# Two banks in turn for the dense product of a graph layer, and the compare tables moved from PSUM to SBUF

## The chip, the cores and the metric

The kernel runs on one core of a Trainium2 chip, as one program. The metric is the time of one execution on the device, in microseconds (us). The engines of the core are TensorE (PE in the rows, and PEld for its weight loads), VectorE (DVE), ScalarE (ACT), GpSimd (POOL) and SyncE (SP). SBUF is the working memory; PSUM has eight banks of 2 KB in each partition, which TensorE writes and which VectorE and ScalarE read.

## The reference

One layer of a graph network with two kinds of edges, then a residual and a layer norm. There are 12,500 nodes of 128 features and 400,000 edges, sorted by their target node.

```
Xs  = X[src]                                   # (400000, 128)
msg = where(edge_types == 0, Xs @ W_data.T + b_data, Xs @ W_control.T + b_control)
agg = segment_sum(msg, dst, num_segments=12500)
h   = relu(agg + (X @ W_self.T + b_self))
out = layernorm(X + h, axis=-1, eps=1e-05)     # no scale, no shift
```

The kernel uses that the sum over edges can come before the products with the weights: for each node and edge kind it sums the source rows, and then multiplies the sums.

## The kernel before

**Three parts of x.** TensorE multiplies two-byte numbers, so x is split in three bf16 parts (high, middle, low). `x3` keeps them side by side in SBUF, 98 blocks of 128 rows by 385 columns (3 x 128 and a column of ones, which counts edges). A copy of them, `x3_dram`, serves the gathers. The split is made in the load phase, up to about 73 us, on ScalarE (L813, L823) and VectorE (L1147, L1163).

**The dense part** covers the first 5632 nodes, in 88 blocks of 64 nodes (x 2 kinds = 128 columns). For a block a matrix of counts is made: how often each of the 12,500 source nodes occurs among the edges of each target and kind. It is made in eight batches. `make_onehots(n)` (VectorE, L1136) compares the keys of edges with tables of running numbers and writes one-hots: `hot_p` (512 two-byte elements in a partition) and `hot_q` (784). `build(n)` (TensorE, L648) multiplies the one-hots into the banks of `build_ps`, in two halves; `evacuate(n)` (ScalarE, L860) copies the counts to `cnt` in two activations. `cnt` holds two blocks in turn. `apply(k, c)` (TensorE, L664) multiplies an eighth of block k's counts with `x3` and adds up all 98 products in one bank, `apply_ps`. Then `post(k)` (VectorE, L1210 and L1211) reads the bank into `zd` and `sd` and raises `posted`. `turn_block(k)` turns the sum two steps later, and `take_block` (ScalarE) stores it.

**The sparse part** covers the other nodes, in 173 rounds of ten tiles of 128 edges. GpSimd gathers the source rows by index (L560), ten gathers a round, into 20 slots, two rounds ahead; within a round it waits at four places for later batches of `build`, so that the gathers are spread out. `make_hot(ps)` (VectorE, L1041) makes a one-hot of the targets inside windows of 32 nodes, by comparing keys with the table `HOT`; in the first 12 rounds it and the gathered rows are float. `gather_sums` (TensorE, L630, in the first 12 rounds L627) sums the rows; `add_parts` (L1191, L1193) and `add_sums` (L1181, L1183) on VectorE bring them to the accumulators.

**Order.** All engines run the same list of 700-odd steps, written out ahead. In a step TensorE does at most one `gather_sums`, one `build`, one small turn or output in the bank `misc`, and one eighth of an `apply`. The x products of block k start at step 8 + 8k. VectorE does the `post` of the block before at the start of the same step, then the sums, then `make_onehots` for three steps later.

**PSUM before.** `const_ps` holds constants (the table `HOT` as floats, and the tables for `hot_p` and `hot_q` as bf16 numbers, each stored twice in a row), `build_ps` takes four banks, `apply_ps`, `sum_ps` and `misc` one each. All eight are in use. The x products of a block wait for the read of the block before:

```
                if c == 0:
                    pe.wait_ge(evacuated, 16 * (k + 1))
                    if k:
                        pe.wait_ge(posted, k)
```

Of the kernel before, what the change touches and what calls it, by code (L numbers as in the profile page):

```python
# [12 lines left out]
ALU = mybir.AluOpType  # L13
# [36 lines left out]
def gnn_resnorm(nc, x, src, dst, etype, w_data, b_data, w_ctrl, b_ctrl, w_self, b_self, out):  # L50
# [116 lines left out]
    with ctx:  # L167
# [20 lines left out]
        hot_p = sb("hot_p", [P, 8, P, 2], BF16)  # L188
        hot_q = sb("hot_q", [P, 8, 2 * XBLOCKS, 2], BF16)
        src_t = sb("src_t", [P, GROUPS * GT], I32)  # L190
        key_t = sb("key_t", [P, GROUPS * GT])
# [64 lines left out]
        def region(b0, nb, dt):  # L256
# [31 lines left out]

        const_ps = psum("const_ps")
        build_ps = [psum(f"build{i}", 2 * WIDE) for i in range(2)]  # L290
        apply_ps = psum("apply_ps")
        sum_ps = psum("sum_ps")
        misc = psum("misc")
        end_ps = [build_ps[1][:, 0:D], build_ps[1][:, WIDE:WIDE + D], build_ps[0][:, WIDE:WIDE + D],
                  apply_ps[:, 0:D]]
        HOT = slice(0, 2 * WIN)
        TABLES = slice(2 * WIN, 2 * WIN + P + 2 * XBLOCKS)
        tables = const_ps[:, TABLES].bitcast(BF16).rearrange("p (w r) -> p w r", r=2)
        table_p, table_q = tables[:, 0:P, :], tables[:, P:P + 2 * XBLOCKS, :]
        twice = start_hot[:, :, :].rearrange("p k n -> p (k n)").bitcast(BF16)[:, 0:2 * (P + 2 * XBLOCKS)].rearrange(  # L300
            "p (w r) -> p w r", r=2)

# [281 lines left out]
        def _(pe):  # L584
# [24 lines left out]
            for k in range(3):  # L609
                last = pe.transpose(apply_ps[:, k * D:(k + 1) * D], w_nat[:, k, :], ident[:, :])  # L610
            last.then_inc(weights_turned, 1)
# [40 lines left out]
            def apply(k, c):  # L652

                if c == 0:
                    pe.wait_ge(evacuated, 16 * (k + 1))
                    if k:
                        pe.wait_ge(posted, k)
                    if k == 0:
                        pe.wait_ge(wt_ready, 1)
                b0, b1 = XBLOCKS * c // 8, XBLOCKS * (c + 1) // 8  # L660
                if k == 0:
                    pe.wait_ge(x3_ready, -(-b1 // XB))
                for b in range(b0, b1):
                    last = pe.matmul(apply_ps[:, 0:385], cnt[:, k % 2, b, :], x3[:, b, 0:385],  # L664
                                     start=(b == 0), stop=(b == XBLOCKS - 1))
                if c == 7:
                    last.then_inc(applied, 1)
# [100 lines left out]
            with pe.If(general > 0):  # L768
                with pe.Fori(0, TILES) as t:
                    pe.wait_ge(late_gathered, (t + 1) * 16)  # L770
                    pe.transpose(misc[:, 0:P], late_x, ident[:, :]).then_inc(late_turned, 1)
                    pe.wait_ge(late_xt_ready, t + 1)
                    pe.matmul(apply_ps[:, 0:2 * D], late_xt, w_t[:, 1:3, :].rearrange("p k d -> p (k d)"),
                              start=True, stop=True).then_inc(late_both_ready, 1)
                    with pe.Fori(0, WINDOWS) as w:
                        pe.wait_ge(late_hot_ready, t * WINDOWS + w + 1)
                        pe.matmul(sum_ps[:, 0:LW], late_msg, late_hot, start=True, stop=True
                                  ).then_inc(late_summed, 1)
                pe.wait_ge(late_added, TILES * WINDOWS)
                for u in range(LATE_UNITS):  # L780
                    i = UNITS + u
                    r = late_rows(u)
                    pe.wait_ge(y_ready, i)
                    pe.wait_ge(late_bias_loaded, 32 + 16 * (u + 1))
                    pe.transpose(misc[:, 0:r], x_u[0:r, 1, :], ident[0:r, 0:r]).then_inc(late_turned, 1)
                    pe.wait_ge(late_xt_ready, TILES + u + 1)
                    pe.matmul(apply_ps[0:r, 0:D], x_t[:, 1, 0:r], w_t[:, 0, :], start=True, stop=False)
                    pe.matmul(apply_ps[0:r, 0:D], acc_all[:, u * P:u * P + r], ident[:, :],
                              start=False, stop=False)
                    pe.matmul(apply_ps[0:r, 0:D], fin_deg[:, 0, 0:r], bias3[:, :], start=False, stop=True  # L790
                              ).then_inc(late_both_ready, 1)
# [3 lines left out]
        def _(act):  # L795
# [102 lines left out]
            for c in range(FIRST_X):  # L898
                split_hi(c)
                if c:  # L900
                    split_mid(c - 1)
                if c == 1:
                    act.wait_ge(weights_turned, 1)
                    act.activation(w_t[:, :, :].rearrange("p k d -> p (k d)"), apply_ps[:, 0:3 * D],
                                   ACT.Copy).then_inc(wt_ready, 1)
                if c == 2 or c == 3:
                    store_lists(c - 1)
# [59 lines left out]
        def _(dve):  # L967
# [53 lines left out]
            dve.wait_ge(iota_done, 5)  # L1021
            dve.tensor_copy(const_ps[:, HOT], hot_i[:, :])
            twice_p, twice_q = twice[:, 0:P, :], twice[:, P:P + 2 * XBLOCKS, :]
            for r in range(2):
                dve.tensor_copy(twice_p[:, :, r], iota_q[:, 0:P])
                last = dve.tensor_single_scalar(twice_q[:, :, r], iota_q[:, :], 1.0, ALU.add)
            step(last)
            dve.tensor_copy(const_ps[:, TABLES], twice.rearrange("p w r -> p (w r)").bitcast(F32))
            step(dve.tensor_copy(iota_n[:, :], iota_i[:, :]))

            def make_hot(ps):
# [5 lines left out]
                elif 2 * ps % P == 0:  # L1037
# [3 lines left out]
                dve.tensor_tensor(to[:, ps % 3, :, :],  # L1041
                                  const_ps[:, HOT].unsqueeze(1).to_broadcast([P, 2 * GT, 2 * WIN]),
                                  keys.unsqueeze(2).to_broadcast([P, 2 * GT, 2 * WIN]),
# [161 lines left out]
            def post(k):  # L1205

                dve.wait_ge(applied, k + 1)
                if k:
                    dve.wait_ge(misc_full, job[block_step[k - 1]] + 1)
                dve.tensor_tensor(zd[:, :], t_mask[:, 1, :], apply_ps[:, 384:385].to_broadcast([P, 2]), ALU.mult)  # L1210
                dve.tensor_reduce(sd[:, :], apply_ps[:, 0:384].rearrange("p (k d) -> p d k", k=3), AX.X, ALU.add  # L1211
                                  ).then_inc(posted, 1)
# [114 lines left out]
            with dve.If(general > 0):  # L1327
# [7 lines left out]
                with dve.Fori(0, TILES) as t:  # L1335
# [6 lines left out]
                    dve.wait_ge(late_both_ready, t + 1)  # L1342
                    dve.tensor_tensor(late_both[:, 0:D], apply_ps[:, 0:D], sd[:, :], ALU.add)
                    dve.tensor_tensor(late_both[:, D:2 * D], apply_ps[:, D:2 * D], late_bias, ALU.add
                                      ).then_inc(late_step, 1)
# [20 lines left out]
                for u in range(LATE_UNITS):  # L1366
                    i = UNITS + u
                    dve.wait_ge(late_both_ready, TILES + u + 1)
                    dve.wait_ge(out_ready, i - 1)
                    residual(i, late_rows(u), apply_ps, 1)  # L1370
                    moments(i, late_rows(u))
# [21 lines left out]
```

## Time and profile before

| | |
|---|---|
| time, median of 3 runs | 2782.12 us (2778.26 to 2785.72) |
| time of the profiled execution | 2784.88 us |
| its span, first to last instruction | 2783.0 us |
| TensorE, matmuls | 2364.6 us busy (85%) |
| GpSimd | 1691.7 us (61%) |
| VectorE | 1266.1 us (45%) |
| ScalarE | 1224.5 us (44%) |
| mean granted clock of TensorE | 0.96 of full speed |

The span is the time in which instructions run; the profiled execution takes 1.9 us more. An engine's busy time is a sum over its instructions. Matmuls are pipelined and their ends are modelled, so the busy time of TensorE is no measure of how near it is to its peak. Idle time of an engine is listed with what ended it; "issue" means that the profile shows nothing that it waited for, "remote" a release that the profile can't place.

### The profile page before, as it was taken

What the parts mean: (1) busy time and instruction counts of PE and PEld (TensorE: products, weight loads), DVE (VectorE), ACT (ScalarE), POOL (GpSimd) and SP (SyncE); (2) the same over time, 40 slices, a digit from 0 to 9 for tenths busy, and PEclk for the clock granted to TensorE, in tenths of its full rate; (3) what the DMA queues carried; (4) which work ended last, traced back from release to release, by engine and by line L of the source; (5) the groups of instructions that cost most, each with busy time, mean ns of one, the idle gap of its engine ahead of it and who ended that gap; (6) DMA issues with size and microseconds to landing.
All of it is one profiled execution on the core that took longest, in us unless ns stands there. A gap on an engine that the chain in (4) does not pass through costs nothing.

```text
span 2783.0 us, 47819 instructions
## 1 busy us (share of the span) xinstructions
PE 2364.6 (85%) x17776; PEld 1301.3 (47%) x17776; DVE 1266.1 (45%) x4037; ACT 1224.5 (44%) x1997; POOL 1691.7 (61%) x1785
## 2 busy tenths in 40 slices
PE   3688888888888888888889888988888888888988
PEld 2344444544444444444445454444444444444444
DVE  8444444445444444444444454444444444444443
ACT  6344444444444444444444444444444444444443
POOL 6466665666666665666666666566666666656662
PEclk9899999999999999999999999999999999999999
DMA  7712222222222222222222222222222222222221
GB/s 191 223 47 67 71 72 59 73 68 74 72 73 71 73 72 62 74 69 75 71 72 73 69 75 71 63 69 73 74 69 73 71 73 72 69 61 72 71 75 34
DMA packets 150380, 211.42 MB, mean 76 GB/s; under 512 B 35298, under 2 KB 120725, under 8 KB 150147
## 3 DMA queue, kind: packets, MB, share of 16 engines
q0 software_dynamic: 83232, 170.57, 22.0%
q1 hardware_dynamic: 54177, 28.15, 3.7%
q10 hardware_dynamic: 12738, 9.60, 1.1%
q8 instruction: 145, 2.38, 0.3%
q14 instruction: 88, 0.72, 0.1%
HBM read 189.78 MB, written 18.41 MB: 75 GB/s over the span
## 4 chain that ended last, share of the span: by engine, by line
PE 44%; another core or an unknown queue 23%; ACT 14%; DVE 9%; issue 7%; DVEq 2%; DMA 1%; SPq 0%; ACTq 0%
PE apply_ps L664 25%; ACT cnt L860 13%; PE build L648 8%; PE sum_ps L630 4%; DVEq L1177 2%; DVE hot_q L1136 2%; DVE hot_p L1136 1%; PE misc L673 1%; DVE acc L1183 1%; PE misc L714 1%; DVE sg L1193 1%; PE misc L717 1%; DMA key_dram<-fin 1%; PE misc L692 1%
## 5 line engine op out<-in xcount | busy, mean ns | idle before, releaser
L560 POOL DMA_INDIRECT rows<-x_dram,src_t x1610 | 1524.7, 947 | 947.5 <-issue 383.4
L860 ACT ACTIVATE cnt<-build 128x784 bf16<-128x784 f32 x1408 | 1087.5, 822 | 1457.1 <-remote 773.1
L664 PE MATMUL apply_ps<-x,cnt 128*128 128x385 bf16 x8624 | 1611.2, 337 | 31.0 <-issue 25.5
L664 PEld LDWEIGHTS apply_ps<-x,cnt 128*128 128x128 bf16 x8624 | 868.3, 103 | 604.7 <-issue 135.7
L648 PE MATMUL build<-hot_q,hot_p 64*128 64x196 bf16 x5632 | 425.1, 254 | 274.2 <-ACT cnt L860 205.6
L648 PEld LDWEIGHTS build<-hot_q,hot_p 64*128 64x128 bf16 x5632 | 197.6, 95 | 572.7 <-issue 372.7
L1136 DVE TENSOR_TENSOR hot_q<-const_ps,key_pq 128x784 bf16<-128x784 bf16 x704 | 390.3, 554 | 0.0
L1181 DVE TENSOR_TENSOR acc_deg<-misc,acc_deg 2x32 f32 x346 | 61.9, 179 | 671.2 <-remote 278.7
L1136 DVE TENSOR_TENSOR hot_p<-const_ps,key_pq 128x512 bf16<-128x512 bf16 x704 | 291.2, 414 | 43.1 <-DVE acc L1183 16.5
L560 POOL DMA_INDIRECT rows<-in_x,src_t x120 | 122.8, 1024 | 76.8 <-issue 30.5
L1191 DVE TENSOR_TENSOR zg<-t_mask,sum_ps 128x2 f16<-128x2 f32 x161 | 24.9, 154 | 307.5 <-PE sum_ps L630 158.3
L630 PE MATMUL sum_ps<-rows,hot 128*64 128x385 bf16 x1610 | 162.5, 331 | 0.0
L1216 DVE SCALAR_TENSOR_TENSOR y_sb<-misc,x_u 128x128 f32<-128x128 f32 (+3 forms) x105 | 30.4, 290 | 268.1 <-PE misc L717 163.9
L1041 DVE TENSOR_TENSOR hot<-const_ps,key_t 128x640 bf16<-128x640 f32 (+1 forms) x173 | 140.9, 814 | 0.0
L630 PEld LDWEIGHTS sum_ps<-rows,hot 128*64 128x64 bf16 x1610 | 77.1, 108 | 76.7 <-issue 52.1
L1193 DVE TENSOR_REDUCE sg<-sum_ps 128x128 f32<-128x384 f32 x161 | 88.7, 551 | 0.0
L1183 DVE TENSOR_TENSOR acc<-misc,acc 128x64 f32 x346 | 77.7, 225 | 2.1 <-issue 2.1
L1210 DVE TENSOR_TENSOR zd<-t_mask,apply_ps 128x2 f16<-128x2 f32 x88 | 13.6, 155 | 127.2 <-remote 45.6
L673 PE MATMUL misc<-ident,sg 128*128 128x128 f32 x173 | 58.8, 340 | 0.0
L692 PE MATMUL misc<-ident,x_u 128*128 128x128 f32 (+3 forms) x105 | 35.0, 333 | 27.1 <-DVEq L1186 14.3
L672 PE MATMUL misc<-picks,zg 128*2 128x64 f16 x173 | 33.2, 192 | 25.9 <-DVEq L1099 19.4
L537 POOL DMA_INDIRECT key_raw<-key_dram,key_at x44 | 41.8, 949 | 21.5 <-issue 13.1
(182 smaller groups left out, 1082.5 us busy)
## 6 DMA issues: line engine op xcount, KB each, us to landing
rows<-x_dram,src_t POOLq DMA_INDIRECT x1610
x_dram<-x ACTq DMA_DIRECT2D x13, 672.0 KB
cnt<-in_x SPq DMA_DIRECT2D x13, 448.0 KB
x_u<-in_x SPq DMA_DIRECT2D x43, 64.0 KB
out<-out_sb SPq DMA_DIRECT2D x43, 64.0 KB
key_dram<-fin SPq DMA_DIRECT2D x12, 196.5 KB
x_u<-in_x SPq DMA_DIRECT2D x40, 53.5 KB
out<-out_sb SPq DMA_DIRECT2D x40, 53.5 KB
```

Of the source, the lines that this page charges most:

```text
L560: pool.indirect_dma_start(out=rows_f[:, slot, 0:D] if early else rows[:, slot, 0:ROW], out_offset=None, in_=x if early else x3_dram, in_of ...
L630: last = pe.matmul(sum_ps[part, 0:ROW + 1], hot_b[:, ps % 3, st, :], rows[:, slot, 0:ROW + 1], start=(j == 0), stop=(j == GT - 1))
L648: last = pe.matmul(build_ps[z][:, o:o + 2 * XBLOCKS], hot_p[half, slot, :, i], hot_q[half, slot, :, i], start=True, stop=True)
L664: last = pe.matmul(apply_ps[:, 0:385], cnt[:, k % 2, b, :], x3[:, b, 0:385], start=(b == 0), stop=(b == XBLOCKS - 1))
L673: pe.transpose(misc[:, 0:P], sg[:, ps % 2, 0:D], ident[:, :]).then_inc(misc_full, 1)
L692: pe.transpose(misc[:, 0:v.r], x_u[0:v.r, i % 3, :], ident[0:v.r, 0:v.r]).then_inc(misc_full, 1)
L860: act.activation(o, i.rearrange("p h (m b) -> p b h m", b=XBLOCKS), ACT.Copy).then_inc(evacuated, 1)
L1041: dve.tensor_tensor(to[:, ps % 3, :, :], const_ps[:, HOT].unsqueeze(1).to_broadcast([P, 2 * GT, 2 * WIN]), keys.unsqueeze(2).to_broadcast( ...
L1136: last = dve.tensor_tensor(to[:, z:z + 2, :, :], table.unsqueeze(1).to_broadcast([P, 2, w, 2]), keys.unsqueeze(2).to_broadcast([P, 2, w, 2 ...
L1181: dve.tensor_tensor(dw, misc[0:2, P + 32 * g:P + 32 * g + 32], dw, ALU.add)
L1183: dve.tensor_tensor(aw, misc[:, 64 * g:64 * g + 64].rearrange("p (t w) -> p t w", t=2), aw, ALU.add).then_inc(acc_step, 1)
L1193: dve.tensor_reduce(sg[:, ps % 2, 0:D], sum_ps[:, 0:ROW].rearrange("p (k d) -> p d k", k=3), AX.X, ALU.add).then_inc(sg_ready, 1)
```

## The change

1. `apply_ps` becomes two banks. Block k uses bank k % 2, and its first product waits for the read of block k - 2. `post(k)` reads bank k % 2. All other users take bank 0.
2. `const_ps` goes, which frees the bank for this. The table `HOT` moves to the SBUF tile `hot_t`, the bf16 tables to the SBUF tile `tables`. Both compares, L1136 and L1041, then have two inputs in SBUF: a table and the keys.
3. In the set-up the bf16 tables are written straight into `tables`. Before, they were made in a spare part of `start_hot` and copied to the bank.

The gathers of three parts (rows of 384 two-byte numbers) stay as they are.

```diff
+        hot_t = sb("hot_t", [P, 2 * WIN])
+        tables = sb("tables", [P, P + 2 * XBLOCKS, 2], BF16)
...
-        const_ps = psum("const_ps")
         build_ps = [psum(f"build{i}", 2 * WIDE) for i in range(2)]
-        apply_ps = psum("apply_ps")
+        apply_ps = [psum(f"apply{i}") for i in range(2)]
...
-        tables = const_ps[:, TABLES].bitcast(BF16).rearrange("p (w r) -> p w r", r=2)
         table_p, table_q = tables[:, 0:P, :], tables[:, P:P + 2 * XBLOCKS, :]
...
-                    if k:
-                        pe.wait_ge(posted, k)
+                    if k >= 2:
+                        pe.wait_ge(posted, k - 1)
...
-                    last = pe.matmul(apply_ps[:, 0:385], cnt[:, k % 2, b, :], x3[:, b, 0:385],
+                    last = pe.matmul(apply_ps[k % 2][:, 0:385], cnt[:, k % 2, b, :], x3[:, b, 0:385],
...
-            dve.tensor_copy(const_ps[:, HOT], hot_i[:, :])
-            twice_p, twice_q = twice[:, 0:P, :], twice[:, P:P + 2 * XBLOCKS, :]
+            dve.tensor_copy(hot_t[:, :], hot_i[:, :])
             for r in range(2):
-                dve.tensor_copy(twice_p[:, :, r], iota_q[:, 0:P])
-                last = dve.tensor_single_scalar(twice_q[:, :, r], iota_q[:, :], 1.0, ALU.add)
-            step(last)
-            dve.tensor_copy(const_ps[:, TABLES], twice.rearrange("p w r -> p (w r)").bitcast(F32))
+                dve.tensor_copy(table_p[:, :, r], iota_q[:, 0:P])
+                dve.tensor_single_scalar(table_q[:, :, r], iota_q[:, :], 1.0, ALU.add)
             step(dve.tensor_copy(iota_n[:, :], iota_i[:, :]))
...
-                                  const_ps[:, HOT].unsqueeze(1).to_broadcast([P, 2 * GT, 2 * WIN]),
+                                  hot_t[:, :].unsqueeze(1).to_broadcast([P, 2 * GT, 2 * WIN]),
...
-                dve.tensor_tensor(zd[:, :], t_mask[:, 1, :], apply_ps[:, 384:385].to_broadcast([P, 2]), ALU.mult)
-                dve.tensor_reduce(sd[:, :], apply_ps[:, 0:384].rearrange("p (k d) -> p d k", k=3), AX.X, ALU.add
+                dve.tensor_tensor(zd[:, :], t_mask[:, 1, :], apply_ps[k % 2][:, 384:385].to_broadcast([P, 2]), ALU.mult)
+                dve.tensor_reduce(sd[:, :], apply_ps[k % 2][:, 0:384].rearrange("p (k d) -> p d k", k=3), AX.X, ALU.add
                                   ).then_inc(posted, 1)
```

## Rows read from the trace of the kernel before

**Rows 1.** The page, busy time of each engine over the span

```profile
PE 2364.6 (85%) x17776; PEld 1301.3 (47%) x17776; DVE 1266.1 (45%) x4037; ACT 1224.5 (44%) x1997; POOL 1691.7 (61%) x1785
```

**Rows 2.** The page, the chain that ended last, by engine and by line

```profile
PE 44%; another core or an unknown queue 23%; ACT 14%; DVE 9%; issue 7%; DVEq 2%; DMA 1%; SPq 0%; ACTq 0%
PE apply_ps L664 25%; ACT cnt L860 13%; PE build L648 8%; PE sum_ps L630 4%; DVEq L1177 2%; DVE hot_q L1136 2%; DVE hot_p L1136 1%; PE misc L673 1%; DVE acc L1183 1%; PE misc L714 1%; DVE sg L1193 1%; PE misc L717 1%; DMA key_dram<-fin 1%; PE misc L692 1%
```

**Rows 3.** Groups by line and form: count, busy us, mean ns, idle before

```profile
L664 PE MATMUL apply_ps<-x,cnt 128*128 128x385 bf16 x8624 | 1611.2, 337 | 31.0 <-issue 25.5 <-DVE sd L1211 4.0 <-ACT cnt L860 1.4
...
L1136 DVE TENSOR_TENSOR hot_q<-const_ps,key_pq 128x784 bf16<-128x784 bf16 x704 | 390.3, 554 | 0.0
L1136 DVE TENSOR_TENSOR hot_p<-const_ps,key_pq 128x512 bf16<-128x512 bf16 x704 | 291.2, 414 | 43.1 <-DVE acc L1183 16.5 <-remote 8.7 <-issue 7.7
L630 PE MATMUL sum_ps<-rows,hot 128*64 128x385 bf16 x1610 | 162.5, 331 | 0.0
L1041 DVE TENSOR_TENSOR hot<-const_ps,key_t 128x640 bf16<-128x640 f32 x161 | 131.1, 814 | 0.0
```

**Rows 4.** Timeline around 1530: start, duration, engine, operation, idle before

```profile
1528.36 2.31 PE L664 MATMUL apply_ps<-x,cnt 128*128 128x385 bf16 x13
...
1530.60 1.01 PE L630 MATMUL sum_ps<-rows,hot 128*64 128x385 bf16 x10
...
1532.91 0.16 DVE L1210 TENSOR_TENSOR zd<-t_mask,apply_ps 128x2 f16<-128x2 f32 x1 [1.70 <-remote]
1532.99 0.55 DVE L1211 TENSOR_REDUCE sd<-apply_ps 128x128 f32<-128x384 f32 x1
1533.14 1.54 ACT L860 ACTIVATE cnt<-build 128x784 bf16<-128x784 f32 x2 [3.92 <-PE build L648]
...
1533.69 2.14 PE L664 MATMUL apply_ps<-x,cnt 128*128 128x385 bf16 x12 [0.98 <-issue]
...
1535.76 0.53 PE L648 MATMUL build<-hot_q,hot_p 64*128 64x196 bf16 x8
```

**Rows 5.** Timeline around 1258, TensorE and then ScalarE

```profile
1258.54 2.14 PE L664 MATMUL apply_ps<-x,cnt 128*128 128x385 bf16 x12 [2.25 <-issue]
1260.61 0.53 PE L648 MATMUL build<-hot_q,hot_p 64*128 64x196 bf16 x8
...
1258.00 1.54 ACT L860 ACTIVATE cnt<-build 128x784 bf16<-128x784 f32 x2 [4.13 <-remote]
```

**Rows 6.** Waits of TensorE: total us, times, longest us

```profile
PE build L648 <- ACT cnt L860: 205.6, 296, 4.8
...
PE apply_ps L664 <- issue: 25.5, 24, 2.2
```

**Rows 7.** Timeline in the load phase, VectorE and then GpSimd

```profile
41.81 1.13 DVE L1147 TENSOR_TENSOR cnt<-cnt,x 128x896 f32<-128x896 f32 x1
42.89 1.07 DVE L1163 TENSOR_TENSOR x<-cnt,x 128x896 bf16<-128x896 f32 x1
...
41.82 0.95 POOL L560 DMA_INDIRECT rows<-in_x,src_t  x1 [0.30 <-issue]
43.07 1.70 POOL L560 DMA_INDIRECT rows<-in_x,src_t  x1 [0.30 <-issue]
```

**Rows 8.** Timeline around 1526, compares and one gather

```profile
1525.60 0.81 DVE L1041 TENSOR_TENSOR hot<-const_ps,key_t 128x640 bf16<-128x640 f32 x1
1525.78 0.95 POOL L560 DMA_INDIRECT rows<-x_dram,src_t  x1 [0.81 <-PE build L648]
...
1526.66 0.55 DVE L1136 TENSOR_TENSOR hot_q<-const_ps,key_pq 128x784 bf16<-128x784 bf16 x1
```

**Rows 9.** Timeline of GpSimd, one round of ten gathers

```profile
1502.85 0.95 POOL L560 DMA_INDIRECT rows<-x_dram,src_t  x1 [0.30 <-issue]
...
1516.44 0.94 POOL L560 DMA_INDIRECT rows<-x_dram,src_t  x1 [0.30 <-issue]
```

**Rows 10.** The gathers: duration ns min/median/max, first and last start

```profile
L560 POOL DMA_INDIRECT rows<-x_dram,src_t x1610: 941/947/1066, 216.7 to 2737.1; - x179
```

More of the change, by code:

```diff
@@ L294, in gnn_resnorm @@
         end_ps = [build_ps[1][:, 0:D], build_ps[1][:, WIDE:WIDE + D], build_ps[0][:, WIDE:WIDE + D],
-                  apply_ps[:, 0:D]]
-        HOT = slice(0, 2 * WIN)
-        TABLES = slice(2 * WIN, 2 * WIN + P + 2 * XBLOCKS)
-        tables = const_ps[:, TABLES].bitcast(BF16).rearrange("p (w r) -> p w r", r=2)
+                  apply_ps[0][:, 0:D]]
         table_p, table_q = tables[:, 0:P, :], tables[:, P:P + 2 * XBLOCKS, :]
-        twice = start_hot[:, :, :].rearrange("p k n -> p (k n)").bitcast(BF16)[:, 0:2 * (P + 2 * XBLOCKS)].rearrange(
-            "p (w r) -> p w r", r=2)
         lists_loaded = [sem(f"lists_loaded{i}") for i in range(len(LISTS))]
@@ L609, in _ @@
             for k in range(3):
-                last = pe.transpose(apply_ps[:, k * D:(k + 1) * D], w_nat[:, k, :], ident[:, :])
+                last = pe.transpose(apply_ps[0][:, k * D:(k + 1) * D], w_nat[:, k, :], ident[:, :])
             last.then_inc(weights_turned, 1)
@@ L772, in _ @@
                     pe.wait_ge(late_xt_ready, t + 1)
-                    pe.matmul(apply_ps[:, 0:2 * D], late_xt, w_t[:, 1:3, :].rearrange("p k d -> p (k d)"),
+                    pe.matmul(apply_ps[0][:, 0:2 * D], late_xt, w_t[:, 1:3, :].rearrange("p k d -> p (k d)"),
                               start=True, stop=True).then_inc(late_both_ready, 1)
@@ L786, in _ @@
                     pe.wait_ge(late_xt_ready, TILES + u + 1)
-                    pe.matmul(apply_ps[0:r, 0:D], x_t[:, 1, 0:r], w_t[:, 0, :], start=True, stop=False)
-                    pe.matmul(apply_ps[0:r, 0:D], acc_all[:, u * P:u * P + r], ident[:, :],
+                    pe.matmul(apply_ps[0][0:r, 0:D], x_t[:, 1, 0:r], w_t[:, 0, :], start=True, stop=False)
+                    pe.matmul(apply_ps[0][0:r, 0:D], acc_all[:, u * P:u * P + r], ident[:, :],
                               start=False, stop=False)
-                    pe.matmul(apply_ps[0:r, 0:D], fin_deg[:, 0, 0:r], bias3[:, :], start=False, stop=True
+                    pe.matmul(apply_ps[0][0:r, 0:D], fin_deg[:, 0, 0:r], bias3[:, :], start=False, stop=True
                               ).then_inc(late_both_ready, 1)
@@ L903, in _ @@
                     act.wait_ge(weights_turned, 1)
-                    act.activation(w_t[:, :, :].rearrange("p k d -> p (k d)"), apply_ps[:, 0:3 * D],
+                    act.activation(w_t[:, :, :].rearrange("p k d -> p (k d)"), apply_ps[0][:, 0:3 * D],
                                    ACT.Copy).then_inc(wt_ready, 1)
@@ L1342, in _ @@
                     dve.wait_ge(late_both_ready, t + 1)
-                    dve.tensor_tensor(late_both[:, 0:D], apply_ps[:, 0:D], sd[:, :], ALU.add)
-                    dve.tensor_tensor(late_both[:, D:2 * D], apply_ps[:, D:2 * D], late_bias, ALU.add
+                    dve.tensor_tensor(late_both[:, 0:D], apply_ps[0][:, 0:D], sd[:, :], ALU.add)
+                    dve.tensor_tensor(late_both[:, D:2 * D], apply_ps[0][:, D:2 * D], late_bias, ALU.add
                                       ).then_inc(late_step, 1)
@@ L1369, in _ @@
                     dve.wait_ge(out_ready, i - 1)
-                    residual(i, late_rows(u), apply_ps, 1)
+                    residual(i, late_rows(u), apply_ps[0], 1)
                     moments(i, late_rows(u))
```

## The prediction

> **What bounds the kernel now.** I read the page's busy line first, then the chain that ended last, then the groups by line and form, then single stretches of the timeline. TensorE is busy 2364.6 us of the 2783.0 us span, far above the 1266.1 us of VectorE, 1224.5 us of ScalarE and 1691.7 us of GpSimd [rows 1]. The chain agrees: 44% of it is TensorE, the product with x at L664 alone 25%, ScalarE's evacuation at L860 13%, VectorE 9% [rows 2]. So what TensorE waits for sets the time, and the other engines matter through the waits that they end.
>
> Two such waits touch this change. Before the first x product of a block, TensorE idles 31.0 us in all, of which only 1.4 us is put down to the evacuation [rows 3]. The stretches show what the part called "issue" is: at 1532.7 TensorE has finished its last turn, VectorE reads the products of the block before (zd at 1532.91, sd until 1533.54), and only at 1533.69 do the products of the new block start, 0.98 us idle [rows 4]. Near 1258 the same takes 2.25 us [rows 5]. The reason is the one bank: `apply(k, 0)` waits for `posted`. The read itself is late because its release arrives late: the old products end at 1530.67 (2.31 us from 1528.36), and zd starts at 1532.91, 2.2 us later.
>
> The second wait is the build waiting for the evacuation: 205.6 us in 296 waits [rows 6]. The change does not touch it, and it is where time freed before L664 can go.
>
> **Part 1: x products in two banks.** Nothing is added: same 8624 matmuls, same 88 pairs of zd and sd, other addresses. The wait of block k is now for the read of block k-2, which is some 30 us old at that point, so it should cost nothing. Ceiling: 31.0 - 1.4 = 29.6 us [rows 3]. What is late next? In the first stretch, the following build starts at 1535.76 and needs both evacuations, which ran 1533.14 to 1534.68. There is 1.08 us to spare, so the 0.98 us are kept whole. In the second, the build at 1260.61 needs the evacuations that end at 1259.54: 1.07 us of the 2.25 us are kept, or somewhat more where the second half is later [rows 4, 5]. Together they keep 2.05 of 3.23 us, or 63%. The first kind is the commoner one: 24 waits share 25.5 us and the longest is 2.2 us, a mean of 1.06 us [rows 3, 6]. Keeping 98% of a typical wait and half of a long one, I take 75% as the share: 29.6 x 0.75 = 22 us. The bounds of this term are 0 (every microsecond moves to the evacuation wait) and 30 us.
>
> VectorE gets no new wait. The read of block k stays where it was in its program, and `turn_block` still comes two steps later. TensorE may now run ahead of the read, but no further than the evacuations let it.
>
> **Part 2: tables to SBUF, VectorE's own time.** The instructions are hot_p (414 ns), hot_q (554 ns), 704 of each, and hot (814 ns), 161 plus 12 of the float form [rows 3]. Their second input, the keys, lies in SBUF already; now both inputs do. What does the place of an input cost? The float compare of 640 elements from the bank takes 814 ns; the float subtraction of 896 with both inputs in SBUF takes 1.07 to 1.13 us [rows 3, 7]. Taking elements off at the slope between the two, (1.07 - 0.814)/256 = 1.0 ns each, both leave a fixed 0.17 us. So I take no change, 0 us. The two-byte compares do 784 elements in 554 ns and 512 in 414 ns, which is 0.51 ns an element: two at a time, from a bank. Their form is kept, so I keep the rate. If it were lost, each step would pay (512 + 784) x 0.5 = 0.65 us, 704 x 0.65 = 457 us of VectorE time; bounds 0 to 457 us of engine time, of which little is on the path.
>
> The Trainium skill (VectorE: DVE Perf Modes, section "The perf-mode tier table") says that a tensor_tensor reads two-byte data two at a time from SBUF but one at a time when an operand is in PSUM. By that rule, as an estimate from its figures, hot_q should take over 0.9 us now and little more than half of it with this change. The trace has 554 ns already, so the measurement decides, and no gain is counted.
>
> **Part 3: tables to SBUF, GpSimd.** This is the cost to look for. In the load phase VectorE runs instructions with both inputs in SBUF, and there the gathers show what that does. The subtraction L1163 starts at 42.89 and ends at 43.96; the gather that starts under it, at 43.07, lasts 1.70 us in place of 0.95 and ends 0.81 us after the subtraction [rows 7]. In contrast, the compare L1041 from the bank starts at 1525.60 and the gather of 1525.78 keeps its 0.95 us [rows 8]. So a gather that begins under a VectorE instruction with two SBUF inputs waits for its end. After the change every compare is of that kind.
>
> The size: the compares are busy 291.2 + 390.3 + 131.1 = 813 us, 29% of the span [rows 3]. So some 29% of the 1610 gathers [rows 10], about 470, begin under one. The extension is what is left of the compare less 0.14 us (0.81 after its end against 0.95 in all); with half a compare left (0.2 to 0.4 us) that is 0.15 to 0.25 us, or 70 to 120 us of GpSimd over the kernel, 0.6 us in a round of ten gathers. If a waiting gather is passed over by compares that follow at once, it waits for the rest of a run. The run from the hot of 1525.60 to the end of the hot_q at 1527.21 lasts 1.6 us [rows 8], and a pair may stand before it; half of it is 0.8 us, and I take 0.9 us: 420 us in all, or 2.6 us a round.
>
> What hides it: the ten gathers of one round go out from 1502.85 to 1517.38, and TensorE adds them up at 1530.60 [rows 4, 9]. That is over 13 us to spare, and TensorE's sums L630 show no idle at all before them [rows 3]. A round lasts 15.7 us on average (from 216.7 to 2737.1 us, 1610 gathers, 161 rounds [rows 10]), and ten gathers 1.25 us apart (0.95 and 0.30) need 12.5 us [rows 9], so even 2.6 us more fit. I take 0 us on the path.
>
> The Trainium skill (SBUF — State Buffer, section "Who interferes with whom") gives the rule behind these rows: VectorE with two SBUF inputs holds a read port that GpSimd needs as well, and the second to come waits in full. The trace agrees (1.70 us for 0.95). Its list also supposes that a tensor_tensor doesn't stall descriptor making; here L1163 does.
>
> The other way round, L1147 starting 0.01 us before a gather takes 1.13 us, where L1163 with as many elements takes 1.07 [rows 7]. At 0.06 us for the few compares that begin in so narrow a window, 5% of 1581, this is 5 us of VectorE time, 0 on the path; if all paid it would be 95 us, of which the 9% share of VectorE on the chain [rows 2] makes 9 us. In the set-up one copy of 324 words goes (0.5 us at the rate above) with the wait in front of it: taken as 1 us.
>
> **Sum.** -22 (waits) - 1 (set-up) + 0 = -23 us. The profiled execution took 2784.9 us, 1.9 above its span: 2762. The median of runs is 2782.1, 2.8 less, which gives 2759; as the small charges on VectorE and GpSimd can only add, I say 2761.
>
> **Rivals.**
> *The wait only moves.* Releases from TensorE come late, as zd shows (2.2 us after the products' end [rows 4]); if the pause before L664 is what lets them catch up, ScalarE starts its evacuation just as much later and the build waits instead. For it: 205.6 us of build waits [rows 6], and the 4.13 us that ScalarE idles until 1258.00 while TensorE is idle too [rows 5]. Against it: the spare 1.08 us. Time: 0 to 8 us gained, 2778. Chance 0.24.
> *GpSimd becomes the bound (slower).* One mechanism: gathers starved by runs of compares. It decides once a round costs more than 15.7 us, that is 3.2 us more than 12.5. If half the gathers meet a run at 0.9 us, it is 4.5 us a round, 1.3 us too much, x 161 = 209 us slower; just past the point, 0.1 to 0.3 us a round is 16 to 48 us, around 2815. For it: the 1.70 us of [rows 7]. Against: 2.6 us is my upper estimate and 13 us of lead absorb short rounds. Chance 0.10.
> *VectorE slower.* The compares lose their two-at-a-time rate or wait for GpSimd more than thought. Their 3% of the chain (83 us) [rows 2] would grow by 0.65/0.97 = 67%, +56 us, less 23 gained: 2815. Chance 0.05.
> *The change does more than the sum.* TensorE never pauses, the long waits are kept whole too, and VectorE's chain moves up: 35 to 45 us, 2742. Chance 0.08.
> Forecast: 0.53.
>
> **Numbers.** A change of under 0.3%, 8 us, can't be told from none here. The forecast's own range is 2752 to 2772. To leave out no more than 2 in 10 the range must take in the moved wait (up to 2782 and a little of the slower side) and half of the larger gain: 2742 to 2788. Faster: 0.50 of the forecast, 0.08 of the larger gain, 0.05 of the moved wait: 0.63. Same: 0.19 of the moved wait, 0.03 of the forecast's slow edge, 0.02 where a small cost on GpSimd cancels the gain: 0.24. Slower: 0.08 + 0.05 = 0.13.
>
> **What would show it.** Right: idle before L664 falls from 31.0 us to under 4; zd still starts up to 2 us after its products, now without TensorE waiting; gathers in the steady part have a mean above 1.0 us and a maximum of 1.3 us or more, with none before the sums L630; hot_p and hot_q stay at 414 and 554 ns within 15. The wait of the build for L860 grows from 205.6 us by under 10. Wrong: that wait grows by 20 us or more (moved), idle appears before L630 (GpSimd), or the compares' means rise.

## The result: slower, and the profile after

The changed kernel takes 2802.8 us (median of 3, 2799.3 to 2806.2) against 2782.1 us before: a ratio of 1.0075, 95% interval 1.0045 to 1.0104. It is 20.7 us slower, where 21 us faster was forecast; the time lies outside the range.

Three more groups by line and form of the kernel before, to be read with [rows 3]:

```profile
L560 POOL DMA_INDIRECT rows<-x_dram,src_t x1610 | 1524.7, 947 | 947.5 <-issue 383.4 <-remote 270.3 <-PE build L648 159.6
L860 ACT ACTIVATE cnt<-build 128x784 bf16<-128x784 f32 x1408 | 1087.5, 822 | 1457.1 <-remote 773.1 <-PE build L648 643.6 <-issue 37.2
...
L648 PE MATMUL build<-hot_q,hot_p 64*128 64x196 bf16 x5632 | 425.1, 254 | 274.2 <-ACT cnt L860 205.6 <-issue 45.0 <-DVE hot_q L1136 17.2
```

The busy times of the engines and then the same groups of the kernel after. The lines have moved: L660 is L664 of before, L644 was L648, L1129 was L1136, L1034 was L1041, L626 was L630, L556 was L560, L856 was L860.

```profile
PE 2385.4 (85%) x17776; PEld 1307.5 (47%) x17776; DVE 1275.1 (45%) x4036; ACT 1222.2 (44%) x1997; POOL 1781.5 (64%) x1785
...
L660 PE MATMUL apply<-x,cnt 128*128 128x385 bf16 x8624 | 1633.3, 340 | 2.2 <-issue 2.2
L556 POOL DMA_INDIRECT rows<-x_dram,src_t x1610 | 1609.4, 1000 | 888.5 <-issue 402.4 <-remote 250.7 <-PE sum_ps L626 127.2
...
L644 PE MATMUL build<-hot_q,hot_p 64*128 64x196 bf16 x5632 | 426.9, 256 | 306.7 <-ACT cnt L856 223.3 <-issue 53.8 <-DVE hot_q L1129 24.1
L1129 DVE TENSOR_TENSOR hot_q<-tables,key_pq 128x784 bf16<-128x784 bf16 x704 | 393.8, 559 | 0.0
L1129 DVE TENSOR_TENSOR hot_p<-tables,key_pq 128x512 bf16<-128x512 bf16 x704 | 294.1, 418 | 41.7 <-DVE acc L1176 17.3 <-issue 7.3 <-remote 6.6
...
L626 PE MATMUL sum_ps<-rows,hot 128*64 128x385 bf16 x1610 | 164.1, 333 | 0.0
L1034 DVE TENSOR_TENSOR hot<-hot_t,key_t 128x640 bf16<-128x640 f32 x161 | 131.7, 818 | 0.0
```

Read singly, nearly every step of the prediction is there. The idle time before the x products fell from 31.0 to 2.2 us [rows 3]. The compares kept their durations (559, 418 and 818 ns for 554, 414 and 814). The gathers run 85 us longer in all (1609.4 for 1524.7), and the sums L626 never wait. Yet the kernel is slower, and the build idles 306.7 us before its matmuls in place of 274.2; its wait for ScalarE grew from 205.6 us [rows 6] to 223.3 us. In the profiles the mean granted clock of TensorE went from 0.960 to 0.947, and its busy time from 2364.6 [rows 1] to 2385.4 us. Its idle time over the span is the same, 418.4 us before and 419.0 us after.

What the gathers do now can be seen around 1506 in the timeline of the kernel after (start, duration, engine, operation). The gather of 1506.04 begins under the compare L1034, which ends at 1506.47, and itself ends at 1507.29, 0.82 us later: the rule of [rows 7]. The next one begins under two-byte compares and takes 1.32 us.

```profile
1505.68 0.79 DVE L1034 TENSOR_TENSOR hot<-hot_t,key_t 128x640 bf16<-128x640 f32 x1
...
1506.04 1.25 POOL L556 DMA_INDIRECT rows<-x_dram,src_t  x1 [0.30 <-issue]
...
1507.54 0.56 DVE L1129 TENSOR_TENSOR hot_q<-tables,key_pq 128x784 bf16<-128x784 bf16 x1
1507.60 1.32 POOL L556 DMA_INDIRECT rows<-x_dram,src_t  x1 [0.30 <-issue]
```

### The profile page after: what moved, and what is told of

Same layout as the page of the kernel before. It is cut to its first block, busy times and chain, and to the rows that moved or that the text cites. A ratio compares the mean times of both kernels' runs of the same rounds, so it can differ in the third digit from the quotient of the medians.

```text
span 2804.4 us, 47817 instructions
## 1 busy us (share of the span) xinstructions
PE 2385.4 (85%) x17776; PEld 1307.5 (47%) x17776; DVE 1275.1 (45%) x4036; ACT 1222.2 (44%) x1997; POOL 1781.5 (64%) x1785
## 4 chain that ended last, share of the span: by engine, by line
PE 47%; another core or an unknown queue 24%; ACT 14%; DVE 6%; issue 5%; DVEq 2%; SPq 1%; DMA 0%; ACTq 0%
PE apply L660 27%; ACT cnt L856 13%; PE build L644 9%; PE sum_ps L626 4%; DVEq L1170 2%; PE misc L669 1%; DVE hot_q L1129 1%; PE misc L710 1%; DVE hot_p L1129 1%; DVE acc L1176 1%; PE misc L713 1%; DVE sg L1186 1%; PE misc L688 1%; PE misc L712 1%
## 5 line engine op out<-in xcount | busy, mean ns | idle before, releaser
L556 POOL DMA_INDIRECT rows<-x_dram,src_t x1610 | 1609.4, 1000 | 888.5 <-issue 402.4
L856 ACT ACTIVATE cnt<-build 128x784 bf16<-128x784 f32 x1408 | 1087.8, 821 | 1487.5 <-PE build L644 747.6
L660 PE MATMUL apply<-x,cnt 128*128 128x385 bf16 x8624 | 1633.3, 340 | 2.2 <-issue 2.2
L660 PEld LDWEIGHTS apply<-x,cnt 128*128 128x128 bf16 x8624 | 876.9, 104 | 584.3 <-issue 122.4
L644 PE MATMUL build<-hot_q,hot_p 64*128 64x196 bf16 x5632 | 426.9, 256 | 306.7 <-ACT cnt L856 223.3
L644 PEld LDWEIGHTS build<-hot_q,hot_p 64*128 64x128 bf16 x5632 | 197.7, 96 | 608.8 <-issue 397.8
L1129 DVE TENSOR_TENSOR hot_q<-tables,key_pq 128x784 bf16<-128x784 bf16 x704 | 393.8, 559 | 0.0
L1129 DVE TENSOR_TENSOR hot_p<-tables,key_pq 128x512 bf16<-128x512 bf16 x704 | 294.1, 418 | 41.7 <-DVE acc L1176 17.3
L556 POOL DMA_INDIRECT rows<-in_x,src_t x120 | 126.4, 1054 | 71.8 <-issue 31.6
L626 PE MATMUL sum_ps<-rows,hot 128*64 128x385 bf16 x1610 | 164.1, 333 | 0.0
L1034 DVE TENSOR_TENSOR hot<-hot_t,key_t 128x640 bf16<-128x640 f32 (+1 forms) x173 | 141.5, 818 | 0.0
L626 PEld LDWEIGHTS sum_ps<-rows,hot 128*64 128x64 bf16 x1610 | 77.8, 109 | 78.7 <-issue 53.1
L1203 DVE TENSOR_TENSOR zd<-t_mask,apply 128x2 f16<-128x2 f32 x88 | 13.8, 156 | 151.0 <-PE apply L660 84.5
L889 ACT ACTIVATE out_sb<-y_sb,shift,rstd 128x128 f32<-128x128 f32 (+3 forms) x105 | 51.1, 487 | 4.1 <-DVE shift L1222 4.1
```

The lines of the kernel that those rows point to most:

```text
L556: pool.indirect_dma_start(out=rows_f[:, slot, 0:D] if early else rows[:, slot, 0:ROW], out_offset=None, in_=x if early else x3_dram, in_of ...
L626: last = pe.matmul(sum_ps[part, 0:ROW + 1], hot_b[:, ps % 3, st, :], rows[:, slot, 0:ROW + 1], start=(j == 0), stop=(j == GT - 1))
L644: last = pe.matmul(build_ps[z][:, o:o + 2 * XBLOCKS], hot_p[half, slot, :, i], hot_q[half, slot, :, i], start=True, stop=True)
L660: last = pe.matmul(apply_ps[k % 2][:, 0:385], cnt[:, k % 2, b, :], x3[:, b, 0:385], start=(b == 0), stop=(b == XBLOCKS - 1))
L856: act.activation(o, i.rearrange("p h (m b) -> p b h m", b=XBLOCKS), ACT.Copy).then_inc(evacuated, 1)
L1034: dve.tensor_tensor(to[:, ps % 3, :, :], hot_t[:, :].unsqueeze(1).to_broadcast([P, 2 * GT, 2 * WIN]), keys.unsqueeze(2).to_broadcast([P, 2 ...
```

## The experiments

The theories. **A**: the tables cost what is lost, and the two banks gain what was predicted. **B**: the wait before the x products only moved, and the tables are harmless. Two more came with the first answers. **G**: GpSimd's gathers set the time. **H**: TensorE's releases (the semaphore updates by which it tells other engines that a piece of work is done) are held until the gathers in flight have landed.

The runs fell on two kinds of chip, and this matters more than the change. The kernel before took 2782.1, 2806.8 and 2778.5 us on some, and 2317.6, 2314.5 and 2314.1 us on others. I call them the slow and the quick chips. Each ratio below is against the kernel before on the same chip.

### The two parts apart

`tables_only` is the changed kernel with one bank and the old wait:

```diff
-        apply_ps = [psum(f"apply{i}") for i in range(2)]
+        apply_ps = [psum("apply0")] * 2
...
-                    if k >= 2:
-                        pe.wait_ge(posted, k - 1)
+                    if k:
+                        pe.wait_ge(posted, k)
```

`free_bank` is the kernel before, without the wait; so that nothing is overwritten while it is read, VectorE reads the constants in place of the products:

```diff
-                    if k:
-                        pe.wait_ge(posted, k)
...
-                dve.tensor_tensor(zd[:, :], t_mask[:, 1, :], apply_ps[:, 384:385].to_broadcast([P, 2]), ALU.mult)
+                dve.tensor_tensor(zd[:, :], t_mask[:, 1, :], const_ps[:, 0:1].to_broadcast([P, 2]), ALU.mult)
...
-                dve.tensor_reduce(sd[:, :], apply_ps[:, 0:384].rearrange("p (k d) -> p d k", k=3), AX.X, ALU.add
+                dve.tensor_reduce(sd[:, :], const_ps[:, 0:384].rearrange("p (k d) -> p d k", k=3), AX.X, ALU.add
...
```

So `free_bank` leaves the dense sums out of its output. The part of the edit that isn't shown keeps the kernel's own last comparison of edge counts from starting its general path.

`after_again`: 

> The changed kernel once more, beside the others on the same chip. Every theory expects 2795 to 2810 us against about 2782 before, a ratio near 1.0075. It also tells whether the granted clock of 0.947 (0.960 before) comes back: if the clock is the cause of the loss it does; if 0.947 was chance it goes back to 0.96 while the time stays up.

`tables_only`: 

> The changed kernel with one bank for the x products and the old wait for the read of the block before; only the tables lie in SBUF. Theory A (the tables cost: VectorE's compares lock GpSimd out, the gathers run longer): 2805 to 2830 us, slower than the changed kernel or as slow, idle before the x products back near 31 us. Theory B (the wait before the x products only moved, and its loss brings the rest): 2775 to 2790 us, no slower than before, although the gathers have the same long mean of 1.00 us.

`free_bank`: 

> The kernel before, tables still in PSUM, in which VectorE reads the constants' bank instead of the products of x, so that TensorE needs no wait before the x products of a block; the dense sums are thus left out of the output, and the last comparison of edge counts is set to pass. All instructions are as before in number and size. Theory A: 2750 to 2770 us, the 22 to 30 us of the prediction are gained. Theory B: 2782 us or more; idle before L664 is gone, but idle before the build (274.2 us before) grows by as much.

All three ran on a quick chip (before 2317.6 us). `after_again` took 2415.7 us, a ratio of 1.0428 (1.0413 to 1.0442), not the 1.0075 expected; `tables_only` 2414.8 us, 1.0423 (1.0409 to 1.0437); `free_bank` 2312.8 us, 0.9981 (0.9972 to 0.9990). So the tables make the whole loss there, 97 us, and removing the wait gains under 5 us. The second bank gains nothing beside them: `after_again` and `tables_only` differ in it alone, and by 0.9 us. Theory A is right on the tables and wrong on the banks there. Theory B is wrong on the tables; that removing the wait gains little is as it said, but these runs don't show that the wait moved.

The same on other chips, with the changed kernel:

`tables_only_2`: 

> Tables in SBUF, one bank, again, for a chip on which the kernel before takes about 2800 us (on one where it takes about 2318 us the first answer, 1.042, comes again). Theory H (there TensorE's releases are held until the gathers in flight have landed, so that longer gathers make later releases): 1.009, hot_in_sbuf and pairs_in_sbuf added. If it is 1.0075 or less, two banks gained nothing there.

`free_bank_2`: 

> Tables in PSUM, no wait before the x products (the dense sums are left out, as in free_bank). The wait was 31 to 39 us of TensorE's idle time on such chips. The prediction's step: 22 us gained, 0.992. Theory H: the next build waits for a release that comes at the landing of a gather anyway, so the wait moves there: 0.998 to 1.002, idle before the build up by about 30 us.

`after_2`: 

> The changed kernel, beside its two parts on one chip: the product of their ratios, if the parts don't touch each other. 1.0075 on a chip like the first, 1.043 on one like that of after_again.

A quick chip again: 1.0410 (1.0395 to 1.0424), 0.9983 (0.9974 to 0.9992) and 1.0421 (1.0405 to 1.0437). They repeat the first answers and say nothing on slow chips.

`tables_only_3`: 

> Tables in SBUF, one bank. On a chip of about 2800 us, where hot_in_sbuf cost 0.16% and pairs_in_sbuf 0.74%: 1.009 by theory H (later landings, later releases). On a chip of about 2318 us 1.041, as twice before.

`free_bank_3`: 

> Tables in PSUM, no wait before the x products, dense sums left out. On a chip of about 2800 us: the prediction's step says 0.992; theory H says 0.998 to 1.002, with the build's idle time up by what L664's falls. On one of about 2318 us 0.998, as twice before.

Now on a slow chip (before 2778.5 us): `tables_only_3` took 2800.5 us, 1.0069 (1.0054 to 1.0085), and `free_bank_3` 2774.4 us, 0.9997 (0.9979 to 1.0014). The tables cost 19 us, a little less than the 1.009 that was expected. The wait is worth nothing that can be told from zero, and 0.2% (6 us) at the most.

`after_3`: 

> The changed kernel. On a chip of about 2780 us: 1.0069 (the tables, from tables_only_3) times 0.9997 (no wait, from free_bank_3) is 1.0066. On one of about 2318 us 1.042, where the tables alone make 1.041.

It met a quick chip: 2409.5 us, 1.0412 (1.0398 to 1.0426). That the changed kernel is the sum of its parts on a slow chip thus rests on two chips: 1.0075 in the first result against 1.0069 times 0.9997.

### Which compares cost, and on a slow chip

`hot_in_sbuf` moves only the float table of the kernel before:

```diff
-            dve.tensor_copy(const_ps[:, HOT], hot_i[:, :])
+            dve.tensor_copy(hot_t[:, :], hot_i[:, :])
...
-                                  const_ps[:, HOT].unsqueeze(1).to_broadcast([P, 2 * GT, 2 * WIN]),
+                                  hot_t[:, :].unsqueeze(1).to_broadcast([P, 2 * GT, 2 * WIN]),
```

`pairs_in_sbuf` moves only the bf16 tables, as the change does.

`before_again`: 

> The kernel before once more, for its profile on the chip that these runs get: ratio 1.00. In the last group of runs the kernel without any wait before the x products took 2312.8 us and its gathers had a mean of 949 ns. If this chip is as quick, the gathers here have 947 ns, and idle before the sums L630 for gathered rows is near 9 us; if it is like the first one, 2782 us and 0.

`hot_in_sbuf`: 

> The kernel before with the float table of the compare L1041 alone in SBUF; one bank for the x products, the bf16 tables in PSUM. Theory G (GpSimd's gathers pay for each compare that holds them off, and set the time): the cost goes by count times the square of the compare's duration, 161 x 0.814^2 = 107 of 444 in all, 24% of the gathers' 98 us: 24 us slower, a ratio of 1.010, gathers' mean near 962 ns. Theory B (a loss on VectorE or TensorE, GpSimd only a bystander): under 1.004.

`pairs_in_sbuf`: 

> The kernel before with the bf16 tables of hot_p and hot_q alone in SBUF; one bank, the float table in PSUM. Theory G: 76% of the 98 us, 74 us slower, a ratio of 1.032 on a quick chip, gathers' mean near 993 ns. The two parts add up to that of both (1.042). If gathers are passed over by compares in a row, the sum of the two parts falls short of it, since runs are broken up by the compare from the bank.

A slow chip. `before_again` took 2806.9 us, a ratio of 1.0001, with gathers of 948 ns; `hot_in_sbuf` 1.0016 (1.0002 to 1.0029), gathers 951 ns; `pairs_in_sbuf` 1.0074 (1.0050 to 1.0099), gathers 994 ns. The gathers' means rise by 3 and 46 ns, where the count times the square of the duration gave 14 and 45; the pairs agree, the float compare costs less than it gave. By time the pairs carry most of it, as expected, but the sizes were those of a quick chip, and here they are four times too high for the pairs and six times for the float table. Taken by itself, the 1.0016 lies where a loss that doesn't come by way of GpSimd was expected (under 1.004); on this kind of chip it doesn't decide between the two. Idle before the x products was 39.4 us in `before_again`, 23.2 us in `hot_in_sbuf` and 78.4 us in `pairs_in_sbuf`: with one bank and the same wait it changes by tens of us, and the smallest of the three does not belong to the fastest kernel.

### Fewer gathers, and none

`nine_gathers` is the changed kernel with a gather left out of each round:

```diff
+                    if i == 9 and ps >= F32_ROUNDS + AHEAD:
+                        continue
                     pool.indirect_dma_start(
...
+                    if i != 9 or ps < F32_ROUNDS + AHEAD:
                         pe.wait_ge(gathered[slot], 16 * (ps // AHEAD + 1))
```

From round 14 on, the sums of a round then use what the tenth slot holds from before, and are wrong.

`no_gathers` is the kernel before with all row gathers left out from round 14 on, with their waits, so that its sparse sums are wrong too.

`nine_gathers`: 

> The changed kernel with the tenth gather of each round left out from round 14 on (TensorE sums what the slot holds from before, so those sums are wrong), all else as it is. Theory G: GpSimd is what sets the time, a round of nine at 1.31 us is 11.8 us, so TensorE is the bound again: 2300 to 2320 us on a quick chip, ratio 1.00 or a little under, idle before the sums for gathered rows back under 10 us, although the gathers' mean stays near 1010 ns. If the loss comes by another way it stays near 1.04.

`nine_gathers_2`: 

> The changed kernel with the tenth gather of a round left out (sums wrong). On a chip of about 2318 us, theory G (GpSimd sets the time there): back to 2300 to 2325 us, ratio 0.995 to 1.003, no waits for gathered rows before the sums. On one of about 2800 us 0.944 again, since each gather left out brings the landing 1.3 us nearer, some 160 times.

`nine_gathers_3`: 

> The changed kernel without the tenth gather of a round (sums wrong). On a chip of about 2318 us, theory G: TensorE bound again, 0.995 to 1.003. On one of about 2780 us 0.936 to 0.944, as twice before.

On slow chips the ratios are 0.9442 (0.9404 to 0.9480; 2651.3 us) and 0.9363 (0.9344 to 0.9381; 2604.4 us), the second lower than expected; on a quick one 0.9954 (0.9939 to 0.9969; 2303.6 us), as expected.

`no_gathers`: 

> The kernel before without any gather of rows from round 14 on (TensorE sums what the slots hold, so the sparse sums are wrong); GpSimd's gathers of keys stay. Theory H: on a chip with 2800 us the releases of TensorE come at once, as on the other kind, and the time falls to what TensorE needs, 2200 to 2290 us, a ratio of 0.80; ScalarE's waits put down to an unplaced release vanish. If the late releases have nothing to do with gathers, the time stays above 2600 us. On a chip with 2318 us: 2230 to 2290 us, 0.97.

`no_gathers_2`: 

> The kernel before without gathers of rows from round 14 on (sparse sums wrong). On the quick chip it took 2299 us. Theory H: on a chip of about 2800 us it takes about the same 2300 us, a ratio of 0.82, and no late releases are left. If the two kinds of chip differ by TensorE itself, it stays above 2600.

On a quick chip 2299.1 us, 0.9936 (0.9920 to 0.9951), 9 us above what was expected; the slow chip gave 2322.0 us, 0.8354 (0.8337 to 0.8370). That is the run that tells most. Without gathers the two kinds of chip differ by 1%, with them by 20%. On the quick one 2299 us is what the kernel takes without them, and the kernel before lies 15 us above it.

### Two groups of gathers

```diff
-QUARTER = (0, 0, 0, 1, 1, 2, 2, 2, 3, 3)
+QUARTER = (0, 0, 0, 0, 0, 2, 2, 2, 2, 2)
```

`two_groups`: 

> The kernel before with a round's ten gathers in two groups of five (behind two batches of the build) in place of groups of 3, 2, 3 and 2. On a chip of about 2780 us, theory H: TensorE's releases are held through the whole group of 5 x 1.25 + 1 = 7.3 us, in place of 3.5 or 4.8 us, but half as often; a step of about 2.9 us without gathers follows each, so a round takes (7.3 + 2.9) x 2 = 20 us in place of 15.7: slower by 5% or more. If only the number of gathers counts, 0.99 to 1.01. On one of about 2318 us 0.995 to 1.01.

It met a quick chip, 1.0001 (0.9992 to 1.0010), and so tells nothing on theory H. As it equals the kernel before in time there, its profile stands for before on a quick chip.

## Why the prediction was wrong

The sum had two terms that count: 22 us gained before the x products, and 0 us for the longer gathers. Both were wrong. On slow chips, the kind that the forecast was made for, the first is nothing and the second is 19 us of loss; 2761 + 22 + 19 is 2802 us, and 2802.8 us was measured.

**GpSimd's cover (part 3, "what hides it").** This step failed. The mechanism and its size were right: gathers that begin under a compare with two SBUF inputs end 0.82 us after it, and the extension is 85 us in all here, inside the 70 to 120 us given. Wrong was to take 0 us on the path. On slow chips the moved tables cost 19 us, on quick chips nearly the whole extension. Groups by line and form of `two_groups`, where the tables are in PSUM:

```profile
L560 POOL DMA_INDIRECT rows<-x_dram,src_t x1610 | 1522.8, 946 | 499.1 <-issue 476.7 <-PE build L648 12.3 <-PE sum_ps L630 10.1
...
L630 PE MATMUL sum_ps<-rows,hot 128*64 128x385 bf16 x1610 | 167.9, 331 | 8.6 <-DMA rows<-x_dram,src_t 8.3
```

and of `after_3`:

```profile
L556 POOL DMA_INDIRECT rows<-x_dram,src_t x1610 | 1624.6, 1009 | 491.3 <-issue 464.9 <-PE build L644 23.4 <-PE sum_ps L626 3.0
...
L626 PE MATMUL sum_ps<-rows,hot 128*64 128x385 bf16 x1610 | 195.6, 333 | 64.1 <-DMA rows<-x_dram,src_t 63.5
```

and of `nine_gathers_3`:

```profile
L558 POOL DMA_INDIRECT rows<-x_dram,src_t x1451 | 1472.5, 1015 | 521.7 <-issue 412.0 <-PE sum_ps L629 85.6 <-PE build L647 24.0
...
L629 PE MATMUL sum_ps<-rows,hot 128*64 128x385 bf16 x1610 | 163.5, 331 | 1.0 <-DMA rows<-x_dram,src_t 0.9
```

In the first, nearly all idle time of GpSimd is the 0.30 us between gathers ("issue"): it already works without a pause, and any longer gather lengthens its round. The gathers take 102 us longer in `after_3` (1624.6 - 1522.8), and the kernel 95 us (2409.5 - 2314.1), with TensorE now waiting for rows 63.5 us before the sums. Take one gather in ten away, leave the compares as they are, and the loss is gone although each gather still has 1015 ns: GpSimd's sum of gathers set the time. TensorE's clock is not the cause on quick chips: it is 0.985 in `after_3` and 0.986 in `nine_gathers_3`, and the x products take 12 us more in `after_3` (1556.5 for 1544.5 us). By its outcome this was the rival "GpSimd becomes the bound", with a chance of 0.10. Its mechanism was another: gathers passed over by runs of compares, 2.6 us a round and more. The runs show the forecast's own 0.6 us a round (102 us over 161 rounds); only 12 of the 1610 gathers of `after_3` last over 1.8 us. That 0.6 us was enough because the point of decision lay much nearer than the 3.2 us a round that I read: the 15.7 us of a round was not TensorE's own need. On a quick chip a round of `two_groups` lasts 12.9 us, where the ten gathers alone need 12.5 us. The lead of 13 us was no cover either: it absorbs one late round, not a rate.

**TensorE's releases (part 1, the share of 75%).** This step failed on both kinds of chip: of 29.6 us nothing, or 4 to 5 us, is gained. On quick chips there was next to nothing to gain: `two_groups` idles 3.4 us before L664. On slow chips the wait was there, and its removal brings no time. The groups by line and form of `free_bank_3`:

```profile
L662 PE MATMUL apply_ps<-x,cnt 128*128 128x385 bf16 x8624 | 1614.4, 338 | 0.3 <-issue 0.2
...
L648 PE MATMUL build<-hot_q,hot_p 64*128 64x196 bf16 x5632 | 426.3, 254 | 276.1 <-ACT cnt L858 212.1 <-issue 41.7 <-DVE hot_q L1134 16.4
```

The wait for ScalarE is 212.1 us against 182.1 in `before_again` and 205.6 in [rows 6]. The growth asked for by theory H, about 30 us, is met against the one and not the other. All idle time before the build (276.1 us) is only 2 us above the 274.2 us of the kernel before, and 7 us above the 269.0 us of `before_again`. This profile (span 2765.7 us) is also quicker than its own median, and no profile of the kernel before stands beside it on the same chip. So the rows don't show where the freed time went: that the wait moved to the build is argued, not shown. That it is not gained, the ratio settles: 0.9997. The rival "the wait only moves", with a chance of 0.24, had the size (0 to 8 us).

**Why the releases are late.** I saw it (2.2 us between the products' end and zd [rows 4]) and took it as given. Windows of 0.4 us of the kernel before around it, with the busy time of each engine, granted clock, share of the DMA engines busy and GB/s:

```profile
1531.80:1532.20 0.40, 0.40 (x7) 0.23 (x4) 0.00 (x0) 0.00 (x0) 0.00 (x0) 1.00 0.36 82
1532.20:1532.60 0.40, 0.40 (x4) 0.31 (x3) 0.00 (x0) 0.00 (x0) 0.00 (x0) 1.00 0.64 152
1532.60:1533.00 0.40, 0.11 (x1) 0.00 (x0) 0.09 (x2) 0.00 (x0) 0.00 (x0) 1.00 0.57 170
1533.00:1533.40 0.40, 0.00 (x0) 0.00 (x0) 0.40 (x2) 0.26 (x1) 0.14 (x1) 1.00 0.07 22
```

VectorE, ScalarE and GpSimd are all idle from 1531.8 on, though products, sums and build have ended by 1532.1; all three go on between 1532.91 and 1533.26, when the DMA share falls from 0.57 to 0.07, as the gather issued at 1530.79 lands. This is common on this kind of chip. In the trace of the kernel before GpSimd pauses 290 times after a gather (next start 2.3 to 6 us later). The gather's last packet ends 2.26 us after its start (median), and TensorE's first release after the instruction comes 0.13 us before that (median), in 242 of 290 between 0.30 us before and that end. In `before_again` it is 192 of 285, in the kernel after 82 of 168: there the tie is looser. ScalarE tells the same without a look at the packets. Where it had been idle for over 0.3 us, its evacuation starts 1.68 us (median) after the build's last matmul for it in the kernel before, and 0.04 us after it in `two_groups`, on a quick chip, and in `no_gathers_2`, on a slow one. So without gathers the delay goes. The groups of `no_gathers_2`:

```profile
L667 PE MATMUL apply_ps<-x,cnt 128*128 128x385 bf16 x8624 | 1546.2, 328 | 5.1 <-DVE sd L1214 4.3 <-issue 0.8
L863 ACT ACTIVATE cnt<-build 128x784 bf16<-128x784 f32 x1408 | 1082.4, 821 | 998.1 <-PE build L651 935.1 <-issue 33.0 <-remote 29.7
...
L651 PE MATMUL build<-hot_q,hot_p 64*128 64x196 bf16 x5632 | 376.9, 250 | 43.7 <-ACT cnt L863 29.3 <-DVE hot_q L1139 8.3 <-issue 5.1
```

The build idles 43.7 us in place of 274.2 us in the kernel before, and ScalarE's waits that no releaser could be placed for ("remote") are 29.7 us in place of 773.1 us. So on slow chips a step often goes: GpSimd issues two or three gathers, TensorE's releases come when they land, and GpSimd waits for one of them before the next group. If it waited so behind each of the four groups of 3, 2, 3 and 2, a round would take 2 x (2.50 + 2.26) + 2 x (1.25 + 2.26) = 16.5 us. It takes 15.7 us, but that nearness proves little: in the trace of the kernel before GpSimd pauses at 344 of the 644 ends of groups, about two in a round, and some of these pauses are longer.

**The cost on slow chips.** 85 us longer gathers cost 19 us of time there. GpSimd had pauses to give: its idle time before the gathers fell from 947.5 to 888.5 us, which takes up 59 us of the 85. This says where the time went, not why no more was taken up. A gather that waits for VectorE has no packets in flight yet, which may be why it holds the releases so little; that was not tested, and the size stays open.

**The clock, a rival on slow chips.** Between the first two profiles TensorE's busy time grew by 20.8 us and its idle time by 0.6 us, so that the whole loss of 20.7 us lies in slower work at a lower granted clock. From `before_again` to `pairs_in_sbuf`, on one chip, it is 10.7 us (2374.8 to 2385.5) of the 20.7 us between the spans. The granted clock is lower there in nearly all runs: 0.946 to 0.951 in the five of `pairs_in_sbuf`, 0.950 to 0.964 in twenty of the kernel before and 0.953 to 0.961 in those of `hot_in_sbuf`. No run here moves the clock without the gathers, so whether it is a cause of its own or follows from how the longer gathers break up TensorE's work is open.

**The rest.** The durations of the compares (part 2) were right within 5 ns. The Trainium skill (VectorE: DVE Perf Modes, section "The perf-mode tier table") puts a tensor_tensor with an operand in PSUM in its slowest class. The traces do not agree: hot_q takes 554 ns with its table in PSUM and 559 ns with it in SBUF. The 1 us for the shorter set-up was not tested by itself.

No version beats the kernel before in a way that counts: `free_bank` shows 0.2% as the most that a second bank can give on quick chips, and it leaves work out.

## What to carry to other kernels

An engine that is 61% busy, with its users never waiting, can still be the next bound, above all when a fixed pause between its instructions (0.30 us here) isn't counted as busy: divide the time of its work by the period that the true bound needs, not by the period that is measured while something else slows the whole. Before a wait is priced, ask what makes its releaser late; if the next wait may hang on the same late event, count on nothing from removing the first (here 29.6 us of waiting gave 0 to 5 us). Where GpSimd issues the gathers, a table in PSUM can be worth its bank: here VectorE's compares then held no gather off, and on quick chips that was worth 4%.

## What the runs showed of the hardware

- A gather that begins under a VectorE compare with two SBUF inputs ends 0.82 us after the compare (a gather that nothing holds off takes 0.95 us); with one input of the compare in PSUM it is not delayed. The mean of a gather rises from 946 to 1009 ns on quick chips, 947 to 1000 ns on slow ones. The Trainium skill (SBUF — State Buffer, section "Who interferes with whom") states the lock and the trace agrees; its remark that a tensor_tensor does not stall a DMA issued from GpSimd does not hold here.
- The same program took 2314 or 2778 us on different chips. With its gathers left out: 2299 and 2322 us. On the slow kind TensorE's releases come late while gathers are in flight, and often just as one lands: an idle ScalarE starts a median of 1.68 us after the build's end in the kernel before, and 0.04 us in `two_groups` on the quick kind, where gathers follow each other without a pause.

What makes a chip of the one or the other kind stays open.
